# Attention's keys, values and null scores as plain fp32 matmuls on an fp32 copy of the transposed rows, in place of three passes over split operands

## The reference

```python
xn = ln(x, g_norm)                                # layer 0; layer 1 likewise with g_in
q = (xn @ Wq)                                     # 16 heads of 64
kv = xn @ Wkv                                     # one key and one value of 64, shared by the heads
k = concat([null_k, kv[:64]]); v = concat([null_v, kv[64:]])
sim = q . k (+ bias, causal and padding masks)    # layer 0: q and k are normalised to length 1
attn = softmax(sim)                               # over 64 keys and the null key
out = ln((attn @ v) @ Wout, g_out)
```

## Time and profile before

| what | us |
|---|---|
| median of 3 runs | 1522.15 (1520.98 to 1525.44) |
| span of the profiled execution | 1465.9 |
| its own time outside the profile | not given |
| TensorE busy | 1342.3 (92%) |
| VectorE busy | 1123.4 (77%) |
| ScalarE busy | 892.0 (61%) |
| POOL busy | 793.0 (54%) |
| L2011, 384 matmul records, busy | 59.1 |

### The profile page before, as it was taken

The page is one execution under the profiler, slowest core; times in us unless marked ns, Lnnn a source line. Parts: engine busy times, 40 slices in busy tenths (PEclk is TensorE's granted clock), DMA queues, the critical chain, the costliest instruction groups (busy, mean ns, idle before and its releaser), DMA issues.

```text
span 1465.9 us, 43550 instructions
## 1 busy us (share of the span) xinstructions
PE 1342.3 (92%) x15663; PEld 1176.4 (80%) x15664; DVE 1123.4 (77%) x2225; ACT 892.0 (61%) x2229; POOL 793.0 (54%) x836
## 2 busy tenths in 40 slices
PE   4799999999889999889999999878998888999993
PEld 4788988888679999778888888667886667888882
DVE  4798888888845565789999999878885797554557
ACT  3567767776556666646566665557775545555556
POOL 2556656665535454456555564578884005777740
PEclk9799999999999999989999999999997999999996
DMA  8200000000130000000000000010003203333318
GB/s 227 53 7 8 10 8 8 8 10 9 34 81 5 1 0 0 3 9 8 9 9 8 10 7 9 27 53 15 14 14 117 94 2 119 103 101 98 97 41 341
DMA packets 79895, 65.09 MB, mean 44 GB/s; under 512 B 48878, under 2 KB 73457, under 8 KB 78706
## 3 DMA queue, kind: packets, MB, share of 16 engines
q1 hardware_dynamic: 72818, 44.98, 10.6%
q0 software_dynamic: 6912, 17.84, 3.9%
HBM read 39.18 MB, written 18.35 MB: 39 GB/s over the span
## 4 chain that ended last, share of the span: by engine, by line
PE 77%; DVE 10%; issue 5%; ACT 4%; POOL 2%; DMA 1%; SPq 0%; DVEq 0%; ACTq 0%; POOLq 0%
PE psQ L1957 13%; PE psW L2050 12%; PE psQ L2352 8%; PE psW L2331 5%; PE psS L2075 4%; PE psS L2024 4%; PE psT L1986 3%; PE psQ L2153 3%; PE psS L2153 3%; PE psW L2141 3%; PE psM L2141 3%; PE psM L2011 3%; PE psT L2320 1%; PE psM L1975 1%; PE psT L2339 1%
## 5 line engine op out<-in xcount | busy, mean ns | idle before, releaser
L742 POOL TENSOR_TENSOR pn<-ex,rden 128x1024 f32<-128x1024 f32 x64 | 143.8, 2247 | 234.1 <-PE psT L1986 211.7
L1957 PEld LDWEIGHTS psQ<-xT,wq 128*128 128x128 f32 x1536 | 202.8, 202 | 46.3 <-issue 24.2
L1957 PE MATMUL psQ<-xT,wq 128*128 128x256 f32 x1536 | 222.9, 299 | 1.7 <-ACT cur L1067 1.5
L2050 PE MATMUL psW<-wout,oT 128*128 128x256 f32 x1536 | 208.2, 291 | 7.0 <-ACT oT L976 4.8
L2050 PEld LDWEIGHTS psW<-wout,oT 128*128 128x128 f32 x1536 | 193.2, 192 | 13.2 <-ACT oT L976 7.5
L2352 PE MATMUL psQ<-W,exT 128*128 (+1 forms) x624 | 172.6, 412 | 0.0
L782 POOL TENSOR_TENSOR hT<-hf,hT 128x512 fp32r<-128x512 f32 x64 | 85.8, 1340 | 99.4 <-ACT hT L1063 99.2
L862 POOL DMA_INDIRECT rows<-xf,src x72 | 73.1, 1016 | 108.7 <-DVE src L1839 83.4
L2352 PEld LDWEIGHTS psQ<-W,exT 128*128 128x128 f32 x624 | 111.3, 192 | 18.9
L2331 PE MATMUL psW<-W,ehT 128*128 (+1 forms) x624 | 102.7, 301 | 8.3 <-DVE ehT L1869 8.2
L925 ACT ACTIVATE qT<-psQ 128x512 f32<-128x512 f32 x128 | 76.6, 598 | 52.9 <-PE psQ L1957 50.9
(11 more groups left out here) (313 smaller groups left out, 3474.2 us busy)
## 6 DMA issues: line engine op xcount, KB each, us to landing
both<-results SPq DMA_DIRECT2D x8, 1024.0 KB, 12.6
raw_w<-W SPq DMA_DIRECT2D x27, 256.0 KB, 4.1
vv<-vp SPq DMA_DIRECT2D x256, 16.0 KB, 1.8
xf<-xf_all SPq DMA_DIRECT2D x4, 1024.0 KB
out<-X SPq DMA_DIRECT2D x8, 512.0 KB, 5.1
X<-x SPq DMA_DIRECT2D x1, 3584.0 KB, 18.1
bvv<-v_all SPq DMA_DIRECT2D x128, 16.0 KB, 1.8
rows<-xf,src POOLq DMA_INDIRECT x72
```

The lines of the kernel that those rows point to most:

```text
L742: nc.gpsimd.tensor_tensor(pn[:], ex[t % 2][:, :, 0:S], rden[:].unsqueeze(2).to_broadcast([P, H, S]), ALU.mult).then_inc(sem("t_pn"), 1)
L1957: mm = nc.tensor.matmul(psQ[:, cc, h * QT:h * QT + QT], wq[w][:, k, c * P:c * P + P], xT[g % 2][u][:, k, :], start=(k == 0 and j == 0), st ...
L2050: mm = nc.tensor.matmul(psW[:, 0:D], oT[u][:, c, :], wout[w][:, c, :], start=(u == 0 and c == 0 and w == 0), stop=(u == 1 and c == CH - 1))
```

## The change

For each tile ScalarE makes one more copy of the turned rows out of PSUM, whole and in fp32 (`xfull`, four buffers of 128x256), right before it writes the high part of xT. The product with the kvn weights takes this copy and one unsplit fp32 `wkvn`: two matmuls (one for each half of the features) in place of six. The low part of wkvn and VectorE's two subtractions for it in each layer go, and with them their waits. The queries still use the split xT. SBUF places shift: the raw kvn weights get the room of the old low part, and `count` of the feed-forward lies ahead of a hole.

```diff
+XFULL = 4
-        wkvn = [sb("attw", f"wkvn{i}", [P, KD, KVN], F32R) for i in range(2)]
+        wkvn = sb("attw", "wkvn", [P, KD, KVN], F32)
+        region("raw_kvn", 4 * KD * KVN, at=place["attw"][0])
+        place["attw"][0] += 4 * KD * KVN
+        xfull = [sb("work", f"xfull{i}", [P, KD, P], F32) for i in range(XFULL)]
+        count = sb("ffn_work", "count", [P, G4 * D], BF16)
         place["ffn_work"][0] += 8 * K
-        count = sb("ffn_work", "count", [P, G4 * D], BF16)
-                     wlo=2 * KD + 1, mask=1)
+                     wlo=KD + 1, mask=1)
...
# ScalarE, split_hi: the weights times the gain
-                    nc.scalar.activation(wkvn[0][:, k, :], raw_kvn[:, k, :], ACT.Copy, scale=gcol[:, k:k + 1]).then_inc(sem("l_whi"), 1)
+                    nc.scalar.activation(wkvn[:, k, :], raw_kvn[:, k, :], ACT.Copy, scale=gcol[:, k:k + 1]).then_inc(sem("l_whi"), 1)
# ScalarE, norm_hi
                     act.wait_ge(sem("t_xTp"), done + t + 1)
+                    reach(act, sem("t_kvp"), done + t - XFULL + 1)
+                    nc.scalar.activation(xfull[t % XFULL][:], x_bank(t).rearrange("p (k q) -> p k q", q=P), ACT.Copy)
                     nc.scalar.activation(xT[g % 2][0][:, :, j * P:j * P + P], x_bank(t).rearrange("p (k q) -> p k q", q=P),
                                          ACT.Copy).then_inc(sem("t_xhi"), 1)
# VectorE: split_kvn_lo and its calls at both layers' starts
-                nc.vector.scalar_tensor_tensor(wkvn[1][:, k, :], raw_kvn[:, k, :], gcol[:, k:k + 1],
-                                               wkvn[0][:, k, :].bitcast(F32), ALU.mult, ALU.subtract).then_inc(sem("l_wlo"), 1)
# TensorE, attention step
-                            pe.wait_ge(sem("l_wlo"), nth(L, "wlo", 2 * KD))
+                            pe.wait_ge(sem("l_whi"), nth(L, "whi", 2 * KD))
                         for k in range(KD):
-                            for j, (u, w) in enumerate(PASSES):
-                                mm = nc.tensor.matmul(psM[:, 0:KVN], xT[g % 2][u][:, k, at], wkvn[w][:, k, :],
-                                                      start=(k == 0 and j == 0), stop=(k == KD - 1 and j == 2))
+                            mm = nc.tensor.matmul(psM[:, 0:KVN], xfull[t % XFULL][:, k, :], wkvn[:, k, :],
+                                                  start=(k == 0), stop=(k == KD - 1))
                         mm.then_inc(sem("t_kvp"), 1)
```

More of the change, by code:

```diff
@@ L440, in build @@
         raw_q = nc.alloc_sbuf_tensor_at("raw_q", [P, KD, INNER], F32, offset=lo_q)
-        raw_kvn = nc.alloc_sbuf_tensor_at("raw_kvn", [P, KD, KVN], F32, offset=lo_kvn)
+        assert place["raw_kvn"][0] == lo_kvn
+        raw_kvn = sb("raw_kvn", "raw_kvn", [P, KD, KVN], F32)
         raw_o = nc.alloc_sbuf_tensor_at("raw_o", [P, CH, D], F32, offset=lo_o)
@@ L1291, in split_q_lo @@
                                                wq[0][:, k, :].bitcast(F32), ALU.mult, ALU.subtract).then_inc(sem("l_wlo"), 1)
-            def split_kvn_lo(L, k):
-                dve.wait_ge(sem("l_whi"), nth(L, "whi", KD + k + 1))
-                nc.vector.scalar_tensor_tensor(wkvn[1][:, k, :], raw_kvn[:, k, :], gcol[:, k:k + 1],
-                                               wkvn[0][:, k, :].bitcast(F32), ALU.mult, ALU.subtract).then_inc(sem("l_wlo"), 1)
             def split_out_lo(L):
@@ L1500, in second_layer @@
             def second_layer(i):
[L1502 to L1505, removed]
+                if i == 0:
                     masks(LAYERS[0])
@@ L1579, in ffn @@
                             split_q_lo(LAYERS[1], k)
-                        for k in range(KD):
-                            split_kvn_lo(LAYERS[1], k)
             ffn_in_lo(0, 0)
@@ L2041, in step @@
                         if t == 0:
-                            pe.wait_ge(sem("l_wlo"), nth(L, "wlo", 2 * KD + 1))
+                            pe.wait_ge(sem("l_wlo"), nth(L, "wlo", KD + 1))
                         pe.wait_ge(sem("t_ohi"), 2 * (done + t) + 2)
```

## The result

| | median us (lowest to highest) | runs |
|---|---|---|
| before | 1524.1 (1517.87 to 1526.35) | 20 |
| after | 1526.22 (1523.05 to 1533.04) | 20 |

The ratio is 1.003, with a 95% interval of 1.0019 to 1.0041: 4.6 us (2.9 to 6.2) by the ratio, 2.1 by the two medians. So the change makes the kernel slower, by an amount on the edge of what can be told from none, and not faster. The profiled execution of the changed kernel took 1533.04 us, the slowest of the twenty.

What follows compares the result with a forecast made beforehand. TensorE was taken to bound layer 0, a loop of TensorE, POOL and VectorE layer 1. Port losses net of the projection's saving, +8, plus +0.3 for the rest gave about +8 on 1522: 1530 us, range 1516 to 1535.

Steps and rivals of the forecast that it cites:

- (a): Layer 0: VectorE's bias addition loses the SBUF port to POOL's pn every second step; 1530 us, 1525 to 1536, chance 0.56.
- The push: Layer 0: ScalarE's added copy moves VectorE's bias addition back 0.26 us, from 0.20 ahead of pn to 0.06 behind.
- (b): Rival, layer 0: VectorE's addition stays ahead of pn, so the projection's saving stands; 1518 us, 1515 to 1520, chance 0.25.
- (c): Rival, layer 0: the addition loses to pn in only a few steps; about 1523 us, chance 0.14.
- The projection's saving: TensorE: four records of 0.125 us replace six matmuls, saving 0.17 us a step, -4.4 us over 26 layer 0 steps.
- (d): Rival: fp32 weights load at half speed, each of 26 steps 0.2 us longer, +5 us; 1527 to 1536, chance 0.05.
- The price of a lost port: Layer 0: when pn goes first, the addition ends 1.95 us later; two steps change by -0.34 plus 1.2 or 0.7.
- reserves of 1.2 and 0.7 us: Layer 0: how early VectorE's low half of oT is done for TensorE's output product, without and with qmx work.
- The count of pairs: Layer 0: 26 steps taken as 13 slow-and-free pairs, +4.7 to +11.2 us in all, middle +8.
- layer 1's loop: Layer 1: cycle through oT, output product, scores, pn and VectorE, without projection or queries; steps forecast unchanged.
- Layer 0's ramp: Layer 0's first steps, half at the lower clock, forecast to save some tenths: -0.3 us.
- work around the span: The 56 us between the profiled span, 1465.9, and the runs' median, 1522.15, taken as untouched by the change.

Runs made afterwards that it cites:

- The copy alone: Kernel before plus ScalarE's fp32 copy ahead of xT high, read by nobody, projection still six matmuls: 1481.91 us, 1.0103 to before.
- forcing the order: Changed kernel, copy left in place, POOL's pn in layer 0 waiting for the next tile's bias addition: 1465.28 us, 0.9986 to before.
- the late copy: Changed kernel with layer 0's copy moved behind the exponential: 1460.63 us, 0.9956 to before; run again 1462.79 us, 0.9957.
- the control: Kernel before, unedited, profiled again in the place where it takes 1468 us: 1467.03 us, one run.
- the half copy: Changed kernel, in layer 0 128 columns copied ahead of xT high and 128 behind the exponential: 1462.88 us, 0.9971 to before.
- the late copy alone: Kernel before plus the unread fp32 copy, in layer 0 behind the exponential, TensorE waiting for kn: 1471.52 us, 1.0023 to before.
- the kernel before with both waits: Kernel before, pn waiting for the next bias addition in layer 0 and the null bias addition in layer 1: 1482.00 us, 1.0097 to before.

## Why the prediction held, point by point

**The mechanism** was forecast (a) and holds. The push is 0.27 at the copy for a predicted 0.26, pn comes first by 0.07 for a predicted 0.06, the addition takes 2.92 us for about 2.8, steps alternate between a slow and a free one. The copy alone brings the alternation (steps of 12.18), moving it late or forcing the order removes it, so the cause is shown and not only argued. Rival (b), the port kept, fell; it is what the late copy makes come true. (c), lost in a few steps only, fell too: up to tile 24 every second step is slow, ten of 26 in one profile and eleven in the other.

**The projection's saving** was given as 0.17 a step (0.07 to 0.23); it is 0.24 to 0.30 at the projection itself (0.70 to 0.46 or 0.40) and 0.19 of the step's length, measured by the pair of kernels that differ in it alone. After the lead of 0.03 a record so costs 0.09 to 0.11 us and not 0.125. Rival (d) is out. The Trainium skill, page "TensorE: Matmul & The Clock Gate", section "Weight-path perf modes", says that the fast weight load, measured at about 2x, is on for 128 weights only if they are not fp32. This trace shows no such difference between fp32 and the split operand's fp32r: four fp32 loads and their matmuls fit in 0.46 us, and the median load is 190 ns for 192. Whether the fp32r loads are fast ones themselves it can't tell.

```profile
L2006 PEld LDWEIGHTS psM<-wkvn,xfull x256: 186/190/338, 29.7 to 935.4; 128*128 128x128 f32 x128
```

**The price of a lost port** was a term that was off. "I take the middle, +8": the two kinds of step had reserves of 1.2 and 0.7 us, and which is hit was left to chance. In both profiles of the changed kernel, in two places, it is the one with the larger reserve (no qmx work), in every pair up to tile 24. A slow step exceeds a free one by 0.75, close to the 0.7 that the prediction worked out for that kind. A pair so costs 22.81 - 22.38 = +0.43 us, where the prediction's terms give -0.34 + 0.7 = +0.36 for this kind and +0.86 for the other. In the kernel with the copy alone it is the other kind (qmx stands between the subtraction and oT in the step that is slow), and the loss there is 0.95, where the prediction would have had 1.2. What picks the kind was not tried. The middle of two exclusive cases was a poor choice for the likeliest value: it fits no execution.

**The count of pairs** was off too. The prediction takes all 26 steps as 13 pairs. In the kernel before, VectorE has no further tile's moments to take from tile 28 on, and the addition leads pn by 0.54 to 0.70 us there, which a push of 0.26 can't turn round. Tile 29, from the timeline of the kernel before:

```profile
355.03 1.23 DVE L1351 TENSOR_TENSOR ex<-ex,bias_t 128x1024 f32<-128x1024 f32 x1
...
355.57 2.45 POOL L742 TENSOR_TENSOR pn<-ex,rden 128x1024 f32<-128x1024 f32 x1 [4.21 <-PE psT L1986]
```

In the changed kernel the losses are at tiles 6, 8, and so on to 24, and in its second profile once more at tile 27. Measured for tiles 5 to 31 are +6.6 and +5.7 us, and they add up so: ten pairs at +0.43 are +4.3; single longer steps among the first twenty, less those of the kernel before, add +3.3 and +1.2; the last six steps are -0.9 and +0.2. That the measured sum lies between the prediction's lower end (+4.7) and its middle (+8) is luck in part: too many pairs were counted, and longer steps that nobody forecast, and whose cause wasn't found, stand in for them.

**The rest**: layer 1's loop unchanged (10.20), as said. For its start and ramp +0.6 had been put; against the control it was +0.6 before its first projection and +0.4 from there to its last. Layer 0's ramp, predicted at -0.3, was +0.1 in one profile and +3.3 in the other, where TensorE's granted clock was 0.52 from 77 to 84 us, the lower of its two levels (1.2 of 2.4 GHz) nearly throughout, for 1.00 in the other three profiles of the two kernels. TensorE had stood still for 2.54 us just before, for 0.96 at the same place of the other profile.

**The sum** was 1530, from 1522.15 and +8. The median is 1526.22. Against the 1524.1 of the twenty runs of before that is +2.1, by the ratio +4.6, and +6.2 by the ratio in the other place: the direction is as forecast, the size is under the +8, and 1526 lies at the lower end of the own range of (a). The slower starting point (1524.1 for 1522.15) brings it 2 us nearer to 1530. The statement that 56 us around the span are "work around the span that nothing here touches" was a wrong reading: only 1.7 us lie around a span, and the rest is that the profile comes from a place with a quicker expert part. It did no harm to the sum, because only differences within layer 0 went into it.

**What stays open.** In the changed kernel (both profiles) and with the copy alone, a few steps are longer by another 0.5 to 1.6 us, and TensorE shows two or three holes of 0.4 to 1.0 us between 90 and 375 us, mostly in the squares of the queries, with nothing in the profile that it waits for. Two such rows of the changed kernel, from the timeline:

```profile
157.19 0.21 PE L1971 MATMUL psW<-ind,sqT 64*64 64x1 f32 x1 [0.66 <-issue]
...
249.65 0.22 PE L1971 MATMUL psM<-ind,sqT 64*64 64x1 f32 x2 [0.93 <-issue]
```

After the second the granted clock falls to the lower level (0.66 over 250 to 255 us), and two steps around it take 12.89 and 12.59. The kernel before and the one with the late copy have no hole over 0.25 there in either of their two profiles, the half copy one of 0.32, the late copy alone two of 0.33 and 0.44. That would fit the lost port, but the kernel before with both waits never loses it in layer 0 and has holes of 0.64 and 0.66. So what makes the holes wasn't found, and that the lost port does is not shown. They are part of the longer steps in the sum above.

## What to carry to other kernels

When operations of two engines exclude each other and start within some tenths of a microsecond of each other, an edit anywhere upstream is worth what it does to that order first and what it saves second: look for the pair, write down the lead, and compare it with each shift that the edit brings. An operation that is added to a queue goes behind the one on which the bound engine's string waits, even if its own operand has been ready for long; here that turned a loss of 0.4% into a gain of 0.4% with the same work done. A wait that forces the order cured layer 0, and in layer 1 it only moved the collision, since the engine that it delays had a second long operation behind: look at what comes after the operation that is held back.

## What the runs showed of the hardware

VectorE's addition and POOL's multiplication, both with both operands in SBUF, exclude each other, and the first keeps the other out, down to a lead of 0.02 to 0.03 us on either side. With VectorE ahead by 0.03 to 0.20 us, its 128x1024 addition takes 1.22 to 1.23 us and POOL's multiplication 2.78 to 2.96; with POOL ahead by 0.07 the two take 2.92 and 1.91. A tiny VectorE operation (128x64, 0.21 us) waits as a large one does: it took 2.17 us behind POOL's masked bias.

A plain fp32 matmul of 144 columns shows as two records, and two of them (four records and loads) take 0.40 to 0.46 us before the next group starts, where six matmuls of the reduced format took 0.70. At this size fp32 is not the slower format once three passes would be needed.

ScalarE's 128x256 copy from PSUM lasts 0.39 us and pushes its successor by 0.27; a copy of half the columns lasts 0.28 and pushes by 0.16.

The changed kernel's expert part took 339 us in one place and 391 in another, while its attention steps agree to 0.01 us.
